# A second PSUM buffer for the per-head projections of an inverse-square-distance attention block

## The reference

```python
P = layernorm(x) @ W_in + b_in          # 16 heads x (Q, K, V, G), 64 columns each
W = (1e-4 + cdist(Q, K)) ** -2          # cdist: sqrt(q2 + k2 - 2 q.k)
W = W / (1e-4 + W.sum(-1, keepdims=True))
H = G * (W @ V)
x = x + H @ W_out + b_out
x = x + layernorm(x) @ sign(weight).T
```

## Time and profile before

| what | value |
| --- | --- |
| median of 3 runs | 5043.28 us (5042.21 to 5057.16) |
| the profiled execution, its time | 5047.26 us |
| its span on the slowest core (core 7) | 5045.7 us |
| spans of the 8 cores | 5034.5 to 5045.7 us |
| granted TensorE clock, mean | 0.643 to 0.645 |
| busy: PE, DVE, ACT | 54%, 43%, 60% |

### The profile page before, as it was taken

How to read it: one execution, slowest core, us unless ns; L and a number is a source line. 1 busy time by engine, 2 the same in 40 slices (tenths; PEclk the granted TensorE clock), 3 DMA queues, 4 the chain that set the end, 5 groups by cost and what they waited for, 6 DMA issues and landing times.

```text
span 5045.7 us, 44906 instructions; the slowest of 8 cores (5034.5 to 5045.7 us)
## 1 busy us (share of the span) xinstructions
PE 2736.3 (54%) x11472; PEld 1049.2 (21%) x11472; DVE 2170.5 (43%) x2630; ACT 3015.6 (60%) x2321; POOL 145.7 (3%) x300
## 2 busy tenths in 40 slices
PE   1156565555655564655556565646465555545536
PEld 0022122221212121212222121212121222211202
DVE  4524444444444444444444444444444444433354
ACT  2107676675757575767667575757576766767100
POOL 0000000000000000000000000000000000000000
PEclk9977575666565665757565656566565756555756
DMA  2200000000000000000000000000000000000311
GB/s 76 64 12 3 1 10 2 9 1 9 2 9 1 9 2 9 2 1 10 2 9 1 9 2 10 1 9 2 9 1 1 10 2 7 1 1 1 101 34 67
DMA packets 41379, 64.11 MB, mean 13 GB/s; under 512 B 12992, under 2 KB 29376, under 8 KB 40128
## 3 DMA queue, kind: packets, MB, share of 16 engines
q1 hardware_dynamic: 31680, 58.79, 3.7%
q0 software_dynamic: 9472, 2.45, 0.3%
HBM read 50.39 MB, written 8.39 MB: 12 GB/s over the span
## 4 chain that ended last, share of the span: by engine, by line
ACT 36%; DVE 25%; PE 20%; issue 11%; DMA 5%; DVEq 1%; ACTq 0%; SPq 0%; POOLq 0%
ACT Ea L494 16%; DVE wb L502 15%; ACT Ebc L497 15%; PE pp L332 7%; PE pA L516 4%; ACT Lb L488 3%; PE pS L479 3%; DMA Wst<-w_in 2%; DMA rsrow<-A_sb 2%; PE pS L816 1%; PE pp L397 1%; PE pS L662 1%; DVE A_sb L529 1%; DVE KQsq L389 1%; DVEq L845 1%
## 5 line engine op out<-in xcount | busy, mean ns | idle before, releaser
L502 DVE TENSOR_TENSOR wb<-Ea,Ebc 128x2048 bf16<-128x2048 f32 x512 | 1173.3, 2292 | 739.3 <-ACT Ebc L497 730.5
L488 ACT ACTIVATE Lb<-pS 128x1024 f32<-128x1024 f32 x1024 | 1020.6, 1012 | 767.1 <-PE pS L479 764.9
L516 PE MATMUL pA<-wb,Vs 128*65 128x512 bf16 x2048 | 839.5, 554 | 883.4 <-DVE wb L502 883.4
L494 ACT ACTIVATE Ea<-Lb 128x2048 f32<-128x2048 f32 x512 | 978.3, 1911 | 333.6 <-DVE wb L502 296.4
L497 ACT ACTIVATE Ebc<-Lb 128x2048 bf16<-128x2048 f32 x512 | 969.5, 1894 | 0.0
L479 PE MATMUL pS<-Qaug,Kaug 66*128 66x512 bf16 x2048 | 913.0, 550 | 56.9 <-POOLq L417 56.4
L516 PEld LDWEIGHTS pA<-wb,Vs 128*65 128x65 bf16 x2048 | 294.4, 144 | 1404.1 <-issue 1376.5
L332 PE MATMUL pp<-XnT,Wbf 128*64 128x512 bf16 x2048 | 535.7, 409 | 92.9 <-DVE Kaug L351 35.3
L363 PEld LDWEIGHTS pp<-Wbf,XnT 128*128 128x128 bf16 x4096 | 280.9, 128 | 315.0 <-issue 295.8
L363 PE MATMUL pp<-Wbf,XnT 128*128 128x64 bf16 x4096 | 309.6, 238 | 34.4 <-DVE Vs L370 32.3
L370 DVE CAST Vs<-pp 128x64 bf16<-128x64 f32 x512 | 113.4, 221 | 498.9 <-PE pp L363 498.9
(11 more groups left out here) (85 smaller groups left out, 1223.7 us busy)
## 6 DMA issues: line engine op xcount, KB each, us to landing
xst<-x SPq DMA_DIRECT2D x32, 512.0 KB, 3.8
Wst<-w_in SPq DMA_DIRECT2D x128, 128.0 KB, 2.1
XT<-xT SPq DMA_DIRECT2D x8, 1024.0 KB, 17.5
y<-XT SPq DMA_DIRECT2D x32, 256.0 KB, 2.3
wst<-w_out SPq DMA_DIRECT2D x8, 512.0 KB, 4.3
wst<-w_ffn SPq DMA_DIRECT2D x8, 512.0 KB, 3.9
Kaug<-k2row POOLq DMA_DIRECT2D x128, 1.0 KB, 1.5
H<-Htmp POOLq DMA_DIRECT2D x32, 64.0 KB, 1.9
```

What stands on the lines that cost most here:

```text
L488: st("scalar", lambda e, ps=ps, sb=(r // 2) % 2, half=r % 2: e.activation(out=Lb[sb][:, half * 1024:half * 1024 + 1024], in_=pS[ps][:], fu ...
L494: st("scalar", lambda e, s=s: e.activation(out=Ea[:], in_=Lb[s % 2][:], func=AF.Exp, scale=-1.0), waits=[(s_c1, 2 * s + 2), (s_c3, s)], in ...
L502: st("vector", lambda e, s=s: e.tensor_tensor(out=wb[s % 2][:], in0=Ea[:], in1=Ebc[:], op=ALU.subtract), waits=[(s_c2, 2 * s + 2), (s_wcon ...
L516: st("tensor", lambda e, hb=hb, stile=stile, ws=s % 2, half=r % 2, k=k, bk=bk: e.matmul(pAb[bk][0:65, :], Vs[hb][:, stile * 65:stile * 65 ...
```

## The change

`pp_cycle` alternates between `pp` and a new tile `pp2` in a bank of its own. The tile is handed to the matmuls and to the eviction as an argument. The first matmul of a group now waits for the eviction of the group before the last.

```diff
+    pp2 = palloc("pp2", [128, 512], F32, side="right")
...
     def pp_cycle(pe_fns, evac_fn, pe_waits=(), ev_waits=(), ev_inc=None):
+        ppt = [pp, pp2][pp_seq[0] % 2]
         pp_seq[0] += 1
         for i, f in enumerate(pe_fns):
             w = list(pe_waits) if i == 0 else []
             if i == 0:
-                w.append((s_ppf, pp_seq[0] - 1))
-            st("tensor", (lambda e, f=f: f(e)), waits=w, inc=s_pp)
-        st("vector", (lambda e, f=evac_fn: f(e)),
+                w.append((s_ppf, max(0, pp_seq[0] - 2)))
+            st("tensor", (lambda e, f=f, ppt=ppt: f(e, ppt)), waits=w, inc=s_pp)
+        st("vector", (lambda e, f=evac_fn, ppt=ppt: f(e, ppt)),
            waits=[(s_pp, s_pp.n)] + list(ev_waits), inc=s_ppf)
...
-                    def f(e, c=c, n=n, cols0=cols0, hb=hb):
+                    def f(e, ppt, c=c, n=n, cols0=cols0, hb=hb):
                         return e.matmul(
-                            pp[0:64, :],
+                            ppt[0:64, :],
...
-    sfree("pA2", "pA")
+    sfree("pp2", "pA2", "pA")
```

More of the change, by code:

```diff
@@ L340, in q_ev, with f @@
         def q_ev(n):
-            def f(e, n=n, hb=hb, h=h):
+            def f(e, ppt, n=n, hb=hb, h=h):
                 return e.tensor_scalar(out=Qaug[hb][0:64, n * 512:(n + 1) * 512],
-                                       in0=pp[0:64, :],
+                                       in0=ppt[0:64, :],
                                        scalar1=bin_sb[0:64, 2 * h:2 * h + 1], scalar2=-2.0,
@@ L361, in proj_head, with f @@
             for c in range(NCH):
-                def f(e, c=c, t=t, hb=hb):
-                    return e.matmul(pp[0:128, 0:64],
+                def f(e, ppt, c=c, t=t, hb=hb):
+                    return e.matmul(ppt[0:128, 0:64],
                                     XnT[:, c * SLEN + t * 128:c * SLEN + (t + 1) * 128],
@@ L367, in proj_head, with v_ev, f @@
                 fns.append(f)
-            def v_ev(e, t=t, hb=hb):
-                return e.tensor_copy(out=Vs[hb][:, t * 65:t * 65 + 64], in_=pp[0:128, 0:64])
+            def v_ev(e, ppt, t=t, hb=hb):
+                return e.tensor_copy(out=Vs[hb][:, t * 65:t * 65 + 64], in_=ppt[0:128, 0:64])
             pp_cycle(fns, v_ev, pe_waits=[(s_wcast, wc_done), (s_xnt, LN1_XNT)])
         def g_ev(n):
-            def f(e, n=n, hb=hb, h=h):
+            def f(e, ppt, n=n, hb=hb, h=h):
                 return e.tensor_scalar(out=Gt[hb][:, n * 512:(n + 1) * 512],
-                                       in0=pp[0:64, :],
+                                       in0=ppt[0:64, :],
                                        scalar1=bin_sb[64:128, 2 * h + 1:2 * h + 2], scalar2=None,
@@ L394, in proj_head, with mm, ev @@
                 sqtn = s_sqt.n
-                def mm(e, sl=sl, scol=scol):
-                    return e.matmul(pp[0:1, :], scol[0:64, :], KQsq[sl][:],
+                def mm(e, ppt, sl=sl, scol=scol):
+                    return e.matmul(ppt[0:1, :], scol[0:64, :], KQsq[sl][:],
                                     start=True, stop=True)
-                def ev(e, sl=sl):
-                    return e.tensor_copy(out=k2row[sl][:], in_=pp[0:1, :])
+                def ev(e, ppt, sl=sl):
+                    return e.tensor_copy(out=k2row[sl][:], in_=ppt[0:1, :])
                 pp_cycle([mm], ev, pe_waits=[(s_sqt, sqtn)],
```

## The result

The changed kernel takes 4972.45 us (median of 8 runs, 4969.04 to 4981.52), the kernel before 5048.21 (8 runs, 5041.22 to 5059.0). The ratio is 0.985, with a 95% interval of 0.9837 to 0.9864: 76 us or 1.5% less. The prediction was 4975, range 4960 to 5008. The profiled execution has a span of 4974.9 us on its slowest core, core 3, where the one before had 5045.7 on core 7; the cores' spans lie 26 us apart now, before 11.

The account below looks back on a forecast made before the run. TensorE's wait for the eviction of the single buffer `pp` was taken to be on the path; head 0's 34 us plus attention's 34.5 gave 68.5 off 5043.3, so 4975 us, range 4960 to 5008.

Parts of the forecast that it names:

- Head 0, Q and K: 12 projection groups of head 0: without the wait, one group every 1.85 us after a cold first; gain 12.6 us.
- Head 0, V: 32 projection groups of head 0: a round trip of 1.06 us covers two groups, 0.53 each; gain 16.5 us.
- the warm case: In head 0's V groups, denser work lifts the clock: 0.44 us a group, gain 19 us.
- Head 0, G: 4 projection groups of head 0: one cold group and three warm, 10.0 us in place of 14.85; gain 4.9 us.
- Q and K slots: Attention, 15 times: second K group starts 0.63 us earlier, 0.60 kept in three long `wb` intervals; gain 1.8 us a head.
- long intervals: Every second `wb` interval in attention's Q, K slots, made late by TensorE's queue: from 7.61 to about 7.0 us.
- G slots: Attention, 15 times: two waits, the first on the path, the second partly hidden by `wb`; gain 0.5 us a head.
- V slots: Attention: these pairs already run at the 6.26 us of the `wb` chain; gain 0.
- Row-sum slots: Attention: a pair's 9.58 us comes from the square (KQsq) standing behind `wb` on VectorE, not from the buffer; gain 0.
- only head 0: Rival: something equally late stands behind the wait in attention, so its 34.5 us stay away; 5009 us, chance 0.13.
- The clock rival: Attention's Q, K and G slots fall to half clock, 3.3 us more a pair; about 5420 us, slower, chance 0.04.

Follow-up runs that it names:

- run on Q, K and G alone: The kernel before with the later wait only for Q, K and G groups in attention, old wait for V, row sums and head 0: 5028.34 us, ratio 0.9945.
- run on head 0 alone: The kernel before with the later wait only in head 0's projections, old wait for all groups spliced into attention: 5015.04 us, ratio 0.992.
- moving the square alone: The kernel before, single buffer kept, with VectorE making the next row-sum group's square one group earlier, ahead of `wb`: 4774.1 us, ratio 0.9455.

## Why the prediction was right

**The total.** 68.5 us were forecast, 76 measured. The mechanism is shown: the wait gives the gain and the second bank alone none, and head 0 and attention each give their part. Two agreements are luck. The time of 4972 lies so near the forecast 4975 because the median of the kernel before came out 5 us higher than the one that the forecast started from (5048.2 against 5043.3); the gain itself was forecast 7.5 us too small. And attention's 2.32 us a head meets the 2.3 of the sum only because the epilogues, forecast at nothing, gave 0.83 where the Q, K and G slots gave 0.64 less than forecast, and pair 0 took back 0.19. Head 0 gave 39 and not 34. In the profiles the rest is in the last stages, where two cores were slower before; on the slowest core those stages weigh 10.8 us and attention only 20.5.

**Head 0, Q and K: 12.6 forecast, 13.6 measured** (36.36 before, 22.74 after). A warm group follows the next at 1.73 us, not 1.85; the second group, in which the clock came up, took 2.00. The 1.85 came from a group with scores behind it. The prediction took a tail of 0.17 off the cold group's 3.59; off the warm group's 1.89 it gives 1.72, the pace measured.

**Head 0, V: 16.5 forecast, 18.7 measured** (34.06 before, 15.39 after). The pace was set by half a round trip, as said, but at the upper clock: 0.455 a group, where the term took 0.53 and named 0.44 as the warm case. The forecast had the mechanism and took the wrong one of its two levels. On all cores of the kernel before the clock falls 1.6 to 4.9 us after the first V group; with the later wait it stays up through all 15.4 us of V, in every version that has it in head 0. V also starts 14.6 us sooner than before, so that no run separates the denser work from the earlier start.

**Head 0, G: 4.9 forecast, 6.9 measured** (14.85 before, 7.97 after), for the same reason: no cold group.

**Q and K slots: 1.8 a head forecast, 1.39 measured.** Three long intervals as forecast, but each 0.50 or 0.51 shorter (medians) and not 0.60. The term that was mis-sized is the earliest start of the second group: 0.44 us after the scores was read off one pair of rows, 0.53 or 0.54 is what the changed kernel shows in 840 of 896 places in heads 1 to 14. That makes 1.5 us; the 8 heads in which the clock dips take the mean to 1.39. In the pair behind a long interval the forecast had TensorE's chain and that of `wb` tie. It is bound by `wb`: Ea at 1182.30 starts 0.09 us after `wb` ended at 1182.21, and the interval there stays 6.27 in the median.

**G slots: 0.5 forecast, 0.27 measured in the mean, 0.51 in the median** (7.69 to 7.18). In 28 of 120 heads the clock comes up too late and the interval is longer than the 7.69 of before, up to 8.35 us; before, 2 heads had that. The size was right and its dependence on the clock left out.

**V slots: 0 forecast, 0.87 measured,** nearly all in the intervals with an epilogue. This is the one term of weight that was put at nothing and was not: "V slots run at 6.26 already: 0" is true of the plain intervals, but the epilogues among them hold matmuls on the chain, and those run at whichever clock the slots before leave them. The waits of the V groups have no part in it (run on Q, K and G alone), nor has head 0's part of the change (run on head 0 alone).

**Row-sum slots: 0 forecast, 0 measured,** and the reason given for it is shown: moving the square alone takes 3.3 us off each of the pairs, and the second buffer adds nothing there.

**The rivals.** Attention gave its share, so "only head 0" is out. The clock rival ("slower") was right in kind and small in size: the clock did fall in the Q and K slots, in 8 of 120 heads, for 1.9 us each, 0.1 us a head in the mean; it would have taken 21 pairs cold throughout. (Its price of 5420 took 20 us for head 0's gain where the sum has 34, which makes 5405; nothing hangs on that.) The Trainium skill ("TensorE: Matmul & The Clock Gate", Part 1, second failure mode) tells of a kernel whose clock swung with short idles between groups; in the Q and K slots that appeared here only as these 8 dips, and in the V slots (pairs 8 to 23) the clock falls 3.2 times a head without the second buffer, 3.9 times with it and 5.6 times with the extra matmuls. The same page's case in which PSUM double-buffering gave nothing isn't this one: here TensorE stood on the path.

## What to carry to other kernels

A wait for a buffer is worth what follows it on the chain: count the waits, then see in each stage which of them another wait hides, here half of those in the Q, K and G slots of attention and all of those in its V slots. The stage that looks slowest may be bound by order, not by buffers: an operation of 0.41 us standing behind a long one in its queue cost 274 us, over three times what the buffer gave. When a stage gets shorter, look at which clock the next stage's matmuls on the chain will find.

## What was not expected of the hardware

- With the later wait the granted clock in head 0's V groups stayed at 1.00 where it had been 0.52, which made them 0.455 us instead of the 0.53 forecast.
- The clock is a coupling between stages: the four pA matmuls of an epilogue took 1.89 us before and 1.02 to 1.89 after, as in the intervals of 13.81 and 12.96 us shown above. The cores lie further apart too: 4948.4 to 4974.9 us after, 5034.5 to 5045.7 before. Core 3, the slowest after, has heads of 271.30 us and core 7, the fastest, 269.63, 15 × 1.67 = 25 us in all. The 1.67 are 0.57 in the epilogues, 0.37 in the Q and K slots, 0.33 in the G slots and 0.41 into and out of pair 0; plain V and row-sum slots are equal.
- With the second buffer the clock dips for about 3 us in the Q and K slots of 8 of 120 heads, at 1.9 us each; before it never did.
- Extra matmuls meant to hold the clock made the kernel 3.8% slower than the changed one (5160.07 to 4972.45), since the clock swung and each of its low phases held the extra work too.
